# Local attention's exponentials: both halves of a tile in one ScalarE instruction each

## What is computed

```python
q = l2norm(q) * qs
k = l2norm(k) * ksc
q, k = rotary_xpos(q, k)
...
sim = jnp.einsum('bhwid,bhwjd->bhwij', bq, bk)      # bq carries the factor 8
...
mask = (i < j) | (i > j + WINDOW) | (j == -1)
sim = jnp.where(mask, -jnp.finfo(sim.dtype).max, sim)
attn = jax.nn.softmax(sim, axis=-1)
out = jnp.einsum('bhwij,bhwjd->bhwid', attn, bv)
```

## Time and profile before

| | us |
|---|---|
| median of 3 runs | 868.1 |
| lowest and highest of them | 867.17 and 868.54 |
| the profiled execution | 866.22 |
| its span, first to last instruction | 864.4 |

### The profile page before, as it was taken

The page is one execution under the profiler, slowest core; times in us unless marked ns, Lnnn a source line. Parts: engine busy times, 40 slices in busy tenths (PEclk is TensorE's granted clock), DMA queues, the critical chain, the costliest instruction groups (busy, mean ns, idle before and its releaser), DMA issues.

```text
span 864.4 us, 15642 instructions
## 1 busy us (share of the span) xinstructions
PE 719.8 (83%) x5368; PEld 467.4 (54%) x5368; DVE 572.0 (66%) x2196; ACT 490.6 (57%) x1121; POOL 373.3 (43%) x416
## 2 busy tenths in 40 slices
PE   5758798797878976788979899779897998879997
PEld 4436464564665745654546565545564664565443
DVE  5776877768755657648776967757776455763623
ACT  4336384563736535455676595695775855554542
POOL 4465645456533445343354554465443234532100
PEclk9888999879886977899989899999899898799999
DMA  8610010100100000101130221210302001004253
GB/s 260 204 43 2 14 43 14 28 17 13 45 13 2 2 0 1 61 24 59 38 80 23 55 65 32 64 30 13 80 26 62 13 26 30 14 19 131 65 136 89
DMA packets 37162, 41.83 MB, mean 48 GB/s; under 512 B 14346, under 2 KB 23772, under 8 KB 36956
## 3 DMA queue, kind: packets, MB, share of 16 engines
q1 hardware_dynamic: 37083, 40.83, 17.3%
HBM read 28.75 MB, written 2.62 MB: 36 GB/s over the span
## 4 chain that ended last, share of the span: by engine, by line
PE 47%; DVE 29%; ACT 11%; POOL 8%; issue 3%; DMA 1%; SPq 0%; DVEq 0%; POOLq 0%; ACTq 0%
PE act_psum L623 5%; PE moe_psum L633 5%; DVE work L1145 4%; PE dve_psum L455 4%; ACT work L877 4%; PE act_psum L722 3%; POOL work L1537 3%; PE dve_psum L526 3%; PE act_psum L516 3%; DVE res_nrm L1125 2%; PE dve_psum L725 2%; PE act_psum L785 2%; DVE work L1168 2%; DVE stats L1115 2%; DVE sumsq L1175 2%
## 5 line engine op out<-in xcount | busy, mean ns | idle before, releaser
L1537 POOL TENSOR_TENSOR work<-work,rinv 128x512 f32<-128x512 f32 (+1 forms) x80 | 87.6, 1110 | 106.6 <-DVE rinv L1135 105.4
L1519 POOL TENSOR_SCALAR rstd<-mv 128x2 f32<-128x2 f32 x72 | 16.8, 234 | 139.0 <-DVE mv L1118 139.0
L1578 POOL TENSOR_TENSOR hT<-hT,work 128x512 f32<-128x512 f32 x32 | 40.7, 1272 | 71.3 <-DVE work L1168 71.3
L455 PE MATMUL dve_psum<-wqkv,hTs 128*128 128x512 f32 x128 | 67.4, 653 | 2.0 <-ACT hTs L1024 2.0
L877 ACT ACTIVATE work<-work,nbias,rnorm 128x128 f32<-128x128 f32 x128 | 61.1, 478 | 0.0
L855 ACT COPY v_loc<-act_psum 77x512 f32<-77x512 f32 (+2 forms) x72 | 41.3, 582 | 34.4 <-PE act_psum L460 16.5
L442 PE MATMUL act_psum<-ident,res_nrm 128*128 128x128 f32 x96 | 26.6, 366 | 37.0 <-DVE res_nrm L1125 37.0
L1520 POOL TENSOR_TENSOR rstd<-rstd,neg_half 128x2 f32<-128x2 f32 x72 | 52.3, 726 | 6.0
L855 ACT COPY hT<-act_psum 128x512 f32<-128x512 f32 (+1 forms) x60 | 31.2, 523 | 39.4 <-PE act_psum L516 21.8
L1164 DVE TENSOR_TENSOR hT<-dve_psum,tab_a 128x512 f32<-128x512 f32 x32 | 22.1, 689 | 44.1 <-PE act_psum L467 26.8
L1584 POOL TENSOR_TENSOR v_loc<-v_loc,rnorm 128x512 f32<-128x512 f32 x32 | 33.3, 1062 | 38.8 <-DVE rnorm L1187 38.8
(11 more groups left out here) (227 smaller groups left out, 2077.7 us busy)
## 6 DMA issues: line engine op xcount, KB each, us to landing
ahead<-cwT_dram SPq DMA_DIRECT2D x128, 64.0 KB, 2.0
v_loc<-v_loc SPq DMA_DIRECT2D x24, 256.0 KB, 3.7
kT<-cwT_dram SPq DMA_DIRECT2D x80, 64.0 KB, 2.1
qT<-cwT_dram SPq DMA_DIRECT2D x48, 64.0 KB, 2.1
wqkv<-in_wqkv_dram SPq DMA_DIRECT2D x2, 768.0 KB
res_nrm<-in_x_dram SPq DMA_DIRECT2D x4, 256.0 KB, 3.1
w_m<-in_w_m_dram SPq DMA_DIRECT2D x1, 1024.0 KB, 8.5
v_loc<-v_loc SPq DMA_DIRECT2D x8, 128.0 KB, 3.1
```

The lines of the kernel that those rows point to most:

```text
L455: nc.tensor.matmul(bank[:], h, attn_w[:, k * INNER:(k + 1) * INNER], start=True, stop=True)\
L1537: nc.gpsimd.tensor_tensor(some, some, by.unsqueeze(2).to_broadcast(list(some.shape)), ALU.mult).then_inc(ready[u], 1)
L1578: nc.gpsimd.tensor_tensor(own, own, partners[u][:, t % 2, k, :], ALU.add).then_inc(turned_ready[u], 1)
```

## The change

The odd half is treated as the even half was. DVE scales and masks the scores of all eight heads. POOL subtracts the maxima of both halves, in two instructions, and each releases `peak_ready`. ACT takes each half with one exponential over 128x512, without bias, scale or sums. DVE adds up the rows of both halves (`sum_and_invert`) and inverts them. `nbias` is no longer made for the local attention, and the semaphore `less_max` and the function `peaks_done` go. The cross attentions compute as before. A tile's masks are still eight instructions.

```diff
-                def exponentials_by_halves(u, number, b, weights, scale_of, whole=()):
+                def exponentials_by_halves(u, number, b, weights, scale_of):
                     for g in range(2):
-                        if g in whole:
-                            act.wait_ge(less_max[u], number - sm_local(0, 0) + 1)
-                            some = weights[:, HALF * g:HALF * g + HALF, :]
-                            nc.scalar.activation(some, some, ACT.Exp).then_inc(exp_done[u], 1)
-                            continue
-                        act.wait_ge(peak_ready[u], peaks_done(number, g))
+                        act.wait_ge(peak_ready[u], half_done(number, g))
...
                     def exp_local(t, u):
-                        def scale_of(i):
-                            h = 2 * (i % HALF) + i // HALF
-                            return rnorm[u][:, t, h:h + 1]
-
-                        exponentials_by_halves(u, sm_local(l, t), t % 2, lprob[u][:, t % 2], scale_of, whole=(WHOLE,))
+
+                        for g in range(2):
+                            act.wait_ge(peak_ready[u], half_done(sm_local(l, t), g))
+                            some = lprob[u][:, t % 2, HALF * g:HALF * g + HALF, :]
+                            nc.scalar.activation(some, some, ACT.Exp).then_inc(exp_done[u], 1)
...
                                 last = mask_and_peak(bank, c * KEYS, mask, lprob[u][:, b, i, :], peak[u][:, b, i:i + 1],
-                                                     rnorm[u][:, t, h:h + 1] if odd == WHOLE else 1.0)
+                                                     rnorm[u][:, t, h:h + 1])
                             last.then_inc(dve_emptied, 1)
-                            if odd == WHOLE:
-                                continue
-                            dve.wait_ge(dve_emptied, dve_item["s_local", l, t, u, odd] + 1)
-                            some = slice(HALF * odd, HALF * odd + HALF)
-                            nc.vector.scalar_tensor_tensor(out=nbias[u][:, b, some], in0=peak[u][:, b, some], scalar=-1.0,
-                                                           in1=rnorm[u][:, t, odd:HEADS:2], op0=ALU.mult, op1=ALU.mult)\
-                              .then_inc(peak_ready[u], 1)
+
+                    def sum_and_invert(t, u):
+                        for g in range(2):
+                            dve.wait_ge(exp_done[u], half_done(sm_local(l, t), g))
+                            some = slice(HALF * g, HALF * g + HALF)
+                            link(nc.vector.tensor_reduce(sums[u][:, t % 2, some], lprob[u][:, t % 2, some, :], AX.X, ALU.add))
+                            nc.vector.reciprocal(rinv[u][:, t % 2, some], sums[u][:, t % 2, some]).then_inc(rinv_ready[u], 1)
...
                         def less_maxima(t, u):
-                            pool.wait_ge(dve_emptied, dve_item["s_local", l, t, u, WHOLE] + 1)
-                            some = lprob[u][:, t % 2, HALF * WHOLE:HALF * WHOLE + HALF, :]
-                            top = peak[u][:, t % 2, HALF * WHOLE:HALF * WHOLE + HALF]
-                            nc.gpsimd.tensor_tensor(some, some, top.unsqueeze(2).to_broadcast([P, HALF, KEYS]), ALU.subtract)\
-                              .then_inc(less_max[u], 1)
+
+                            for odd in range(2):
+                                pool.wait_ge(dve_emptied, dve_item["s_local", l, t, u, odd] + 1)
+                                some = lprob[u][:, t % 2, HALF * odd:HALF * odd + HALF, :]
+                                top = peak[u][:, t % 2, HALF * odd:HALF * odd + HALF]
+                                nc.gpsimd.tensor_tensor(some, some, top.unsqueeze(2).to_broadcast([P, HALF, KEYS]), ALU.subtract)\
+                                  .then_inc(peak_ready[u], 1)
```

More of the change, by code:

```diff
@@ L1132, in invert_sums @@
                         dve.wait_ge(exp_done[u], half_done(number, g))
-                        if weights is not None and g == WHOLE:
-                            link(nc.vector.tensor_reduce(sums[u][:, b, some], weights[:, some, :], AX.X, ALU.add))
                         nc.vector.reciprocal(rinv[u][:, b, some], sums[u][:, b, some]).then_inc(rinv_ready[u], 1)
@@ L1236, in local_attention_steps @@
                     take_scores(1, u)
-                    invert_sums(u, sm_local(l, 0), 0, lprob[u][:, 0])
+                    sum_and_invert(0, u)
                     yield
@@ L1244, in local_attention_steps @@
                         if n + 1 < TILES:
-                            invert_sums(u, sm_local(l, n + 1), (n + 1) % 2, lprob[u][:, (n + 1) % 2])
+                            sum_and_invert(n + 1, u)
                         if n + 2 < TILES:
```

7 lines of the change are left out of this document (1 added, 6 removed).

## The result

| | before | changed |
|---|---|---|
| median, us | 868.54 (11 runs) | 872.08 (11 runs) |
| lowest and highest | 866.63 to 871.37 | 870.75 to 874.99 |
| profiled execution, its span | 866.22, 864.4 | 872.43, 870.6 |

The ratio is 1.0042, 95% interval 1.003 to 1.0055: the change makes the kernel slower by 0.4%, 3.6 us. The forecast was 867.6 and "no change"; the measured time lies inside its range of 863.5 to 872.5, but near the upper end, which the rivals had set and not the forecast. In a second set of runs (6 of the changed kernel, 29 of before) the ratio was 1.0047 [1.0029, 1.0065].

The account below looks back on a forecast made before the run. No engine alone bounds the kernel; the chain changes engine every few microseconds (TensorE 47%, DVE 29%, ACT 11%). Terms -1.6 + 0 + 0.6 + 0 + 0.5 = -0.5 us gave 865.7, plus 1.9 to the median: 867.6 us, range 863.5 to 872.5.

Parts of the forecast that it names:

- Part 1: ACT's odd half as one exponential instead of four, at ten places on the chain: 1.6 us less in sum.
- kind (b): Five places where the exponentials wait for ACT itself: gain 0.4 us, holding in full at three, 1.2 us.
- kind (a): Places where the exponentials wait for POOL, as at tile 1 of the first pass: gain 0.15 us at 2 of 3.
- Parts 2 and 3: On DVE: longer odd masks against the removed nbias, 0; the second sum, 0.6 us more, in the eighth pass.
- Rival 2: DVE takes ACT's place: the second sum delays the masks of tile n+2, no wait absorbing it; 872 us, chance 0.28.
- Part 4: POOL's second subtraction fits into room in POOL's queue: cost 0, up to 1.04 us at places with less room.
- Part 5: DVE and POOL at once: collisions, priced from L1329, might grow by a tenth like POOL's busy time: +0.5 us.
- rival 3: POOL is in the way: new subtractions collide with two-tile products or come late at `add_partners`; 873 us, chance 0.07.

Follow-up runs that it names:

- a_real012: Changed kernel with POOL's second subtraction only in tiles 0 to 2 of each local pass, left out in tile 3: 869.1 us, 1.0019 of the kernel before.
- a_nosub2: Changed kernel without POOL's subtraction of the odd half; the odd exponential waits for DVE's maxima: 866.16 us, 0.9988 of the kernel before.
- a_sum1key: Changed kernel with the odd half's sum taken over one key of 128: 871.39 us, 1.0037 of the kernel before.
- a_tiny: Changed kernel with POOL's second subtraction replaced by work without data, for which the odd exponential doesn't wait: 867.12 us, 0.999 of the kernel before.
- a_tinywait: Changed kernel with POOL's second subtraction replaced by work without data, for which the odd exponential waits: 865.01 us, 0.9978 of the kernel before.
- a_dve3: Changed kernel with tile 3's second subtraction done by DVE behind its maxima, nothing left out: 871.58 us, 1.0048 of the kernel before.
- a_data32: Changed kernel with the second subtraction replaced by one of 128x1024 constants in tiles 0 and 1, nobody waiting: 0.9992 of the kernel before.
- a_data16: Changed kernel with the second subtraction replaced by one of 128x512 constants in tiles 0 and 1, nobody waiting: 0.9989 of the kernel before.
- a_fill32: Changed kernel with the second subtraction replaced by a 128x1024 fill with zeros in tiles 0 and 1, nobody waiting: 0.9984 of the kernel before.
- b_sub2: Kernel before with POOL subtracting the odd maxima too, no nbias, four small exponentials kept: 871.19 us, 1.0043 of the kernel before.
- a_data3: Changed kernel, but in tile 3 POOL's second subtraction works on constants for which nobody waits: 872.18 us, 1.006 of the kernel before.

## Why the prediction was wrong

**Part 1, ACT: right.** The gain of kind (b) is 0.42 us in the second pass. In the table every profile without the second subtraction in tile 3 gains 0.2 to 0.5 us in the second pass, and all but a_real012 gain 0.7 in the fourth. Of kind (a), tile 1 of the first pass took 68.56 - 65.14 = 3.42 us, the 3.42 of the working:

```profile
65.14 2.00 POOL work L1585 x2
...
67.17 0.64 ACT work L895
...
67.83 0.70 DVE sums L1196
...
68.56 0.03 DVE rinv L1197
```

**Parts 2 and 3: right as far as measured.** With the odd sum cut to one key the changed kernel is at 1.0037 instead of 1.0042: some 0.4 us, less than the intervals show, against 0.6 forecast. In the eighth pass the sum and the masks took 0.77 us more in front of `norm_apply`, near the forecast's 0.6; the span from tile 2's first reciprocal to tile 3's, which was to grow by 0.6, grew from 638.66 - 633.10 = 5.56 to 644.71 - 637.76 = 6.95 us, by 1.39, and the other 0.62 are the collision. Rival 2, with 872, named the measured time, but by a mechanism that the runs rule out: with both sums and no second subtraction nothing is lost (a_nosub2), and in a_sum1key 13 us less on DVE changed the time by less than the intervals show. The masks were not tried by themselves.

**Part 4, POOL's queue: right, and beside the point.** Its cost of 0 for the room in the queue is what a_tiny and a_tinywait show, within their intervals.

**Part 5 is the step that failed.** It priced collisions at 0.5 us, from L1329 alone. The second subtraction with its collisions costs 4.5 to 6.0 us: that is how far the changed kernel's ratios, 1.0042 and 1.0047, lie above those of a_nosub2, a_tiny and a_tinywait, 0.9988, 0.9990 and 0.9978. The operation that costs most in the traces is `norm_apply`, a `tensor_scalar` with one tile in SBUF; the trace of before had it in full view, at 1.28 us for four in the eighth pass. The next is `sums_of_rows`, a product of two SBUF tiles like L1329, that the prediction didn't look at. The way to the end was mis-sized as well: part 5 scaled today's 5 us of collisions by POOL's extra tenth, and rival 3 counted 29% of what DVE loses, while a_dve3, where DVE only spends 0.7 us of its own at these places, is as slow as the changed kernel. By the table, changed kernel against a_tinywait: second pass 0.8 to 1.0 us, fourth 1.7, fifth 0.8 to 1.1, eighth 2.9, less 1.2 to 1.4 that come back behind 660. That makes 4.8 to 5.5, but the table also has 3 us between the same two in 150-225, which no meeting explains, so the sum isn't a proof. Without the collisions, with POOL's time and the wait, the change would have gained 0.1 to 0.2% (a_tiny's interval reaches 1.0005, a_tinywait's 0.9996), about the 1.0 us that the forecast had without part 5.

The Trainium skill (SBUF — State Buffer, Who interferes with whom) was quoted in the prediction for products of two tiles. The same section counts `tensor_scalar` among the operations that can take the pair of ports that DVE and GpSimd share. The trace agrees: 1.90 us for 1.10 on DVE and 1.94 for 1.04 on POOL. I had read half of the rule, and the prediction's sentence that the new subtractions can collide only with products such as L1329 is false. Rival 3, at a chance of 0.07, was the mechanism and 873 nearly its time, but by luck: it counted 16 collisions with L1329, where the trace shows few long meetings, four of them with `norm_apply` or `sums_of_rows`.

**Open.** The stretch 150-225 is 3 us shorter in four of the profiles of the table and not in the others, and 255-420 is 2.8 us longer in two; TensorE's granted clock differs there. The clock isn't chance alone: as a mean over all runs of a kernel it is 0.902 for the changed kernel and 0.904 for before, and 0.908 to 0.912 for a_nosub2, a_tiny, a_tinywait, a_data32, a_data16 and a_fill32. So the kernels without the second subtraction, with which I compare, have more of the clock too, and how much of the 4.5 to 6.0 us goes through it isn't known; b_sub2 shows that the loss against before comes without it. Half of the loss, that of tiles 0 to 2, is traced to two places only. Why most derivatives of the changed kernel lose 0.9 to 1.0 us in the fifth pass even without the second subtraction wasn't tried.

## What to carry to other kernels

Before moving an elementwise operation to GpSimd, list what VectorE does while it would run, and take the room in GpSimd's queue as half of the question. Follow a loss to the end of the program before you price it: of the 2.1 us in the eighth pass 1.4 came back by 765 us, in a stretch where the kernel before had more time at the lower clock. And add a part alone to the old kernel only with the order of the new one in mind: the second sum cost 1.2% by itself and nothing measurable in its place.

## What the runs showed of the hardware

- Four `tensor_scalar` of 128x128 float32 (tile in SBUF, two scalar columns) took 1.10 us alone and 1.90 beside a subtraction of 128x512 on POOL, which took 1.94 instead of 1.04.
- It can be one-sided. In a_tinywait the power of 128x2, with a median of 0.69 us, took 1.50 us beside `norm_apply`, which stayed at 1.11:

```profile
634.25 1.50 POOL L1592 TENSOR_TENSOR spare<-rnorm,neg_half 128x2 f32<-128x2 f32 x1
```

```profile
634.54 1.11 DVE L1112 TENSOR_SCALAR y<-x,mv,rstd 128x128 f32<-128x128 f32 x4
```

- The same subtraction of 128x512 took 0.70 us on DVE (a_dve3) and 1.04 on POOL where it met nothing; the prediction's estimate for DVE was 0.5.
- Two kernels with unlike edits, a_data3 and a_dve3, run in step within 0.1 us from 255 us to the end; in the eighth pass `norm_apply` ends at 643.29 us in one and at 643.23 in the other.
